# Masked attention on one core: one maximum per key tile over two PSUM banks, and a score ring of two banks

## What is computed

```python
q = xt @ Wq.T                       # one matrix for queries, keys and values
scores = scale * jnp.einsum('bhqd,bhkd->bhqk', qh, qh)
logits = (scores * cmask + (1.0 - cmask) * NEG) * rmask
attn = jax.nn.softmax(logits, axis=-1)
ctx = jnp.einsum('bhqk,bhkd->bhqd', attn, qh)
out = ctx @ Wo.T
return x + transpose(out)
```

## Time and profile before

| | |
|---|---|
| median of 3 runs | 1814.85 us (1810.24 to 1817.87) |
| the profiled execution, its own time | 1814.64 us |
| its span, first to last instruction | 1812.8 us |
| instructions in the profile | 40177 |
| PE busy | 1650.4 us, 91% of the span |
| DVE busy | 1306.6 us, 72% |
| POOL busy | 1207.7 us, 67% |
| ACT busy | 851.5 us, 47% |
| mean granted TensorE clock | 0.954 of full speed |
| HBM traffic over the span | 39 GB/s |

### The profile page before, as it was taken

One profiled execution on the slowest core, in us unless ns is written; L12 is line 12 of the kernel. 1 busy time (PEld: TensorE's weight loads), 2 busy tenths in 40 slices (PEclk: granted clock), 3 DMA queues, 4 the chain that ended last, 5 costly groups with the idle time before them and its releaser, 6 DMA issues.

```text
span 1812.8 us, 40177 instructions
## 1 busy us (share of the span) xinstructions
PE 1650.4 (91%) x10956; PEld 1260.7 (70%) x10956; DVE 1306.6 (72%) x2839; ACT 851.5 (47%) x2055; POOL 1207.7 (67%) x1030
## 2 busy tenths in 40 slices
PE   6688989999999999989899998999999899999995
PEld 4566767677767777767767777677776677777763
DVE  5358677786857768696776968678685877769663
ACT  1135455454635545364544636445463554546451
POOL 5357776758667675777757677675866767586752
PEclk8689999999999999999999999999999999999997
DMA  3234353434434353443434434253443434344410
GB/s 102 71 83 116 91 129 78 129 80 116 111 87 118 76 135 86 104 121 92 119 71 127 97 103 120 69 137 77 122 102 89 116 81 131 83 117 103 103 48 27
DMA packets 93863, 179.70 MB, mean 99 GB/s; under 512 B 24704, under 2 KB 24832, under 8 KB 93632
## 3 DMA queue, kind: packets, MB, share of 16 engines
q1 hardware_dynamic: 64448, 109.71, 26.4%
q0 software_dynamic: 29184, 67.17, 12.8%
HBM read 36.77 MB, written 33.55 MB: 39 GB/s over the span
## 4 chain that ended last, share of the span: by engine, by line
PE 61%; DVE 23%; issue 10%; POOL 2%; ACT 2%; DVEq 1%; SPq 0%; DMA 0%; ACTq 0%; POOLq 0%
PE misc L1087 19%; PE ctx_psum L1054 12%; PE max_scores L1026 8%; DVE small_mxp L828 8%; PE scores L1041 6%; DVE small_xsum L823 5%; PE scores L1044 5%; DVE small_rsum L858 3%; PE misc L1145 3%; PE misc L1113 3%; DVE small_ctx L879 2%; DVE small_xcT_lo L850 1%; PE misc L1135 1%; PE misc L1099 1%; PE misc L1133 1%
## 5 line engine op out<-in xcount | busy, mean ns | idle before, releaser
L828 DVE TENSOR_REDUCE small_mxp<-max_scores 108x1 f32<-108x270 f32 x1280 | 538.3, 433 | 330.2 <-PE max_scores L1026 299.9
L698 ACT ACTIVATE small_Pt<-scores,small_kbias 108x270 f32<-108x270 f32 x1280 | 552.9, 485 | 451.0 <-PE scores L1044 425.2
L540 POOL TENSOR_TENSOR small_Pacc<-small_Pacc,small_Pt 108x540 f32<-108x540 f32 x384 | 532.1, 1386 | 266.4 <-ACT small_Pt L698 256.5
L1026 PE MATMUL max_scores<-small_ops 128*108 128x270 f32 x1280 | 413.7, 341 | 79.3 <-DVE small_mxp L828 78.4
L1026 PEld LDWEIGHTS max_scores<-small_ops 128*108 128x108 f32 x1280 | 223.8, 178 | 176.2 <-DVE small_mxp L828 110.0
L1054 PE MATMUL ctx_psum<-small_Pt,small_V 108*64 108x270 f32 x2560 | 322.8, 400 | 0.0
L1041 PE MATMUL scores<-small_ops 128*108 128x270 f32 x1280 | 297.4, 305 | 4.8 <-ACT small_Pt L698 3.9
L858 DVE RECIPROCAL small_rsum<-small_rsum 128x67 f32<-128x67 f32 (+1 forms) x512 | 240.5, 530 | 78.3 <-ACT small_rsum L644 78.3
L1044 PE MATMUL scores<-small_ops 128*108 128x270 f32 x1280 | 270.6, 294 | 0.0
L1054 PEld LDWEIGHTS ctx_psum<-small_Pt,small_V 108*64 108x64 f32 x2560 | 190.8, 141 | 113.9 <-issue 10.2
L492 POOL DMA_INDIRECT small_xg<-x_rows,small_idx_cur x160 | 171.1, 1069 | 103.9 <-POOL small_idx_cur L485 63.3
(11 more groups left out here) (104 smaller groups left out, 2234.0 us busy)
## 6 DMA issues: line engine op xcount, KB each, us to landing
small_ops<-small_H SPq DMA_DIRECT2D x512, 135.0 KB, 2.5
small_ops<-small_L SPq DMA_DIRECT2D x256, 135.0 KB, 2.6
small_xg<-x_rows,small_idx_cur POOLq DMA_INDIRECT x160, 3.6
out_rows<-small_xg,small_idx_cur POOLq DMA_INDIRECT x160, 3.4
small_ops<-small_mrow SPq DMA_DIRECT2D x128, 2.1 KB
wq_sb<-wq SPq DMA_DIRECT2D x1, 1024.0 KB, 5.7
woT_sb<-woT SPq DMA_DIRECT2D x1, 1024.0 KB, 8.2
wqT_sb<-wqT SPq DMA_DIRECT2D x1, 1024.0 KB, 10.2
```

Source lines behind the costliest of these rows:

```text
L540: nc.gpsimd.tensor_tensor(acc, other, t["Pt"][:R, p0], ALU.add).then_inc(pacc_step, 1)
L698: nc.scalar.activation(t["Pt"][:R, (NT * h + k) % f.NP, half, :], ST[(2 * (NT * h + k) + half) % 3][:R, 0:H], ACT.Exp, bias=t["kbias"][:R, ...
L828: nc.vector.tensor_reduce(t["mxp"][:R, h % 2, m // 2, m % 2:m % 2 + 1], MX[m % 2][:R, 0:H], AX.X, ALU.max).then_inc(mx_red, 1)
L1026: nc.tensor.matmul(MX[m % 2][:R, 0:H], ops[:, OPA, tile_cols(m // 2)], ops[:, OPB, half_cols(m % 2)], start=True, stop=True).then_inc(mx_r ...
```

## The change

The PSUM banks are shared out anew: two for scores instead of three, three for maxima instead of two, as one tensor. The two halves of a key tile go to neighbouring banks: tile number NT*h + k even takes banks 0 and 1, odd takes banks 2 and 1, so half 1 (O) is always in bank 1 and half 0 (E) changes between 0 and 2. DVE takes one negated maximum per key tile over both banks, 540 columns, straight into the column of `mcol`. The partial maxima `mxp` and their reduction L833 are gone, and so is their semaphore.

The waits: E of tile k waits for the reduction of tile k - 2, O of tile k for that of tile k - 1. The matmul of score half u waits for the exponential of half u - 2. On DVE part a = 0 of a step has no reduction any more; part a = 1 begins with the one of the whole tile. The index table of the start moves from `ST[2]` to `ST[1]`.

```diff
+SCORE_BANKS, MAX_BANKS = 2, 3
+def same_bank_before(u, banks, per_batch):
+    return u - banks if u >= banks else next(v for v in range(-1, -banks - 1, -1) if (per_batch + v - u) % banks == 0)
...
-        ST = [psum(f"scores{i}", [P, 512], F32) for i in range(3)]
-        MX = [psum(f"max_scores{i}", [P, 512], F32) for i in range(2)]
+        ST = [psum(f"scores{i}", [P, 512], F32) for i in range(SCORE_BANKS)]
+        MX = psum("max_scores", [P, MAX_BANKS, 512], F32)
...
-            keep("mxp", [P, 2, f.NT, 2], F32)
...
-                                                     ST[(2 * (NT * h + k) + half) % 3][:R, 0:H], ACT.Exp,
+                                                     ST[(2 * (NT * h + k) + half) % SCORE_BANKS][:R, 0:H], ACT.Exp,
...
-                def reduce_max(s, h, m):
-                    dve.wait_ge(mx_ready, 2 * NT * s + m + 1)
-                    nc.vector.tensor_reduce(t["mxp"][:R, h % 2, m // 2, m % 2:m % 2 + 1], MX[m % 2][:R, 0:H], AX.X,
-                                            ALU.max).then_inc(mx_red, 1)
-                    if m == 2 * NT - 1:
-                        dve.wait_ge(mx_red, 2 * NT * (s + 1))
+                def reduce_max(s, h, k):
+                    left = (NT * h + k) % 2
+                    dve.wait_ge(mx_ready, 2 * (NT * s + k) + 2)
+                    if k == 0:
                         at_least(dve, mT_ready, s - 1)
-                        nc.vector.tensor_reduce(t["mcol"][:R, h % 2, :], t["mxp"][:R, h % 2], AX.X, ALU.max,
-                                                negate=True).then_inc(mcol_done, 1)
+                    nc.vector.tensor_reduce(t["mcol"][:R, h % 2, k:k + 1],
+                                            MX[:R, left:left + 2, 0:H], AX.XY,
+                                            ALU.max, negate=True).then_inc(mx_red, 1)
...
-                                if h < HEADS - 2 or has_next:
-                                    reduce_max(s + 2, h + 2, 2 * k + a)
+                                if a == 1 and (h < HEADS - 2 or has_next):
+                                    reduce_max(s + 2, h + 2, k)
...
-                    at_least(pe, mx_red, 2 * NT * s + m - 1)
-                    nc.tensor.matmul(MX[m % 2][:R, 0:H], ops[:, OPA, tile_cols(m // 2)], ops[:, OPB, half_cols(m % 2)],
+                    at_least(pe, mx_red, NT * s + m // 2 - 1 + m % 2)
+                    nc.tensor.matmul(MX[:R, 1 if m % 2 else 2 * ((NT * h + m // 2) % 2), 0:H], ops[:, OPA, tile_cols(m // 2)], ops[:, OPB, half_cols(m % 2)],
...
-                        banks.append(ST[u % 3])
-                        last_user = u - 3 if u >= 3 else next(v for v in range(-1, -4, -1) if (count + v - u) % 3 == 0)
+                        banks.append(ST[u % SCORE_BANKS])
+                        last_user = same_bank_before(u, SCORE_BANKS, 2 * NT * HEADS)
                         at_least(pe, exp_done, 2 * NT * (s - h) + last_user + 1)
...
-                        pe.wait_ge(mcol_done, s + 1)
+                        pe.wait_ge(mx_red, NT * (s + 1))
```

More of the change, by code:

```diff
@@ L281, in attention_kernel @@
         whi_done, ctx_hi_done = sem("whi_done"), sem("ctx_hi_done")
-        mx_red, mcol_done, mrow_done, lo_done = sem("mx_red"), sem("mcol_done"), sem("mrow_done"), sem("lo_done")
+        mx_red, mrow_done, lo_done = sem("mx_red"), sem("mrow_done"), sem("lo_done")
         ctx_done, xv_done, xsum_step, mask_step = sem("ctx_done"), sem("xv_done"), sem("xsum_step"), sem("mask_step")
@@ L919, in body @@
                 nc.vector.tensor_tensor(t["idx"][:R, 1:],
-                                        ST[2][:R, NTALL:B * NTALL].rearrange("p (b i) -> p b i", b=B - 1),
+                                        ST[1][:R, NTALL:B * NTALL].rearrange("p (b i) -> p b i", b=B - 1),
                                         t["boff"][:R, 1:], ALU.add).then_inc(idx_made, 1)
@@ L924, in body @@
                     if name == "mT":
-                        for m in range(2 * NT):
-                            reduce_max(0, 0, m)
+                        for k in range(NT):
+                            reduce_max(0, 0, k)
                     job(name, arg, bank, -1 if name == "xT" else 0, 1 if name == "xT" else 0, 0)
                     if name == "mT":
-                        for m in range(2 * NT):
-                            reduce_max(1, 1, m)
+                        for k in range(NT):
+                            reduce_max(1, 1, k)
                     if name == "proj" and arg[0] < 2:
@@ L1007, in body @@
                     for i in range(1, group + 1):
-                        order(g * group + i, ST[2], bass.ds((g * group + i) * NTALL, NTALL))
+                        order(g * group + i, ST[1], bass.ds((g * group + i) * NTALL, NTALL))
                 pe.wait_ge(g_kept, KD)
@@ L1033, in scores @@
                         pe.wait_ge(mrow_put[h % 2], 16 * (s2 + 1))
-                    banks, count = [], 2 * NT * HEADS
+                    banks = []
                     for half in range(2):
                         u = 2 * (NT * h + k) + half
-                        banks.append(ST[u % 3])
-                        last_user = u - 3 if u >= 3 else next(v for v in range(-1, -4, -1) if (count + v - u) % 3 == 0)
+                        banks.append(ST[u % SCORE_BANKS])
+                        last_user = same_bank_before(u, SCORE_BANKS, 2 * NT * HEADS)
                         at_least(pe, exp_done, 2 * NT * (s - h) + last_user + 1)
```

## The result

| | before | after |
|---|---|---|
| median | 1816.15 us (4 runs) | 1846.32 us (4 runs, 1843.25 to 1850.85) |
| ratio, 95% interval | | 1.0181 (1.0162 to 1.0200) |
| span of the profiled execution | 1812.8 us | 1841.5 us |
| mean granted clock | 0.954 | 0.973 |
| DVE busy | 1306.6 us | 1227.1 us |

The account below looks back on a forecast made before the run. It took TensorE's own work to set most of the time (PE busy 91%). Terms: 45 + 8 + 2 - 31 - 2 - 8 = +14 us on 1814.6, so 1829 us; range 1815 to 1844, chance 0.48.

Parts of the forecast that it names:

- The merged reduction: On DVE, 640 reductions of 540 columns at 714 ns each; DVE sheds 102 us, worth nothing where it waits for PE.
- The score ring: Two score banks: a score matmul waits for the step before's second exponential, at least 1.44 us per consecutive light step.
- one miss: An isolated light step whose scores come late for want of a bank: 0.37 us lost.
- The misses at (5,0) and (7,0): Half a score miss at each; with a maximum miss at (5,1) and (7,2), 0.45 us each time.
- Together 2.8 us a batch, 45 us over 16: Sum of score and maximum misses in the light steps of a middle batch, applied to all 16 batches.
- 8 for starts: Ten batch starts without a turn of the loop: two more score misses, 0.8 us each time, 8 us lost.
- 2 for the last batch: Last batch has no maxima in heads 6 and 7, so more light steps: 2 us lost.
- more clock falls: Rival: clock might fall in (6,0) to (6,2), one fall a batch costing 27 us: 1856 us; chance 0.10.
- Head 3: DVE takes the output tile sooner; stall and clock falls go: 31 us gained, plus 2 in batches 0 and 1.
- What is late next is ACT: In head 3, ACT's gathered-tile pass limits the gain: copy at about 879.9, row sums 881.3; 1.85 us taken.
- The turn of the loop: At 5 turns with a long wait, 0.6 us gained and an estimated 1.0 for avoided clock falls: 8 us.
- Cancelled: Rival: half the miss costs return, 1815 us; chance 0.16.

Follow-up runs that it names:

- half by half: On the changed kernel, score matmuls reordered: first and second matmul of half 0, then of half 1; 1806.1 us, 0.9967 of before.

## Why the prediction was wrong

The direction held and so did most unit prices; the size, 14 us against 29, did not.

- *The merged reduction.* 714 ns forecast, 716 measured. That it would be worth little by itself: 1 to 3 us with the scores in the old order, 8 to 10 half by half.
- *The score ring.* 1.44 us from S2 to S2 forecast, 1.45 measured; one miss 0.37 us forecast, 0.37 measured at (2,1). For batches 2 to 13 the forecast's terms make 38 us (12 times 2.8, and 0.8 for six starts), and 45.2 were measured. The forecast has no miss between (2,4) and (3,0), 0.38 a batch and 4.5 us in all, although it removes the stall behind it. The misses at (5,0) and (7,0), which it halves, make another 1.7.
- *The step that failed most* is "Together 2.8 us a batch, 45 us over 16", with 8 for starts and 2 for the last batch, 55 in all; it was 67.2. I priced all 16 batches as a middle one. The first has no output tiles and the last no maxima in its last heads, so they have more light steps: 22.0 us in batches 0, 1, 14 and 15, where the terms make some 16. And (6,2) and (7,2) of the last batch lose 4.2 us to two clock falls that come with the score waits; this is the "more clock falls" rival, in heads 6 and 7 of the last batch alone. The Trainium skill, "TensorE: Matmul & The Clock Gate", section "A second HAM failure mode: psum-queue depth-cycling", says that short idles of PE between groups of matmuls, as the PSUM banks are cycled, can make the clock go to and fro. The trace agrees with that in the last batch, at 4.2 us, and shows none of it in the light steps of heads 5 and 6 of the other batches, where the stretch below keeps its clock:

```profile
929.00:934.50 5.50, 5.39 (x38) 3.33 (x39) 5.33 (x8) 2.52 (x7) 3.56 (x3) 1.00 0.56 124
```

- *Head 3.* 33 us forecast with batches 0 and 1, 40.2 measured, and the clock falls went as forecast. The reason given, the order on DVE, is one of two: with the reductions apart and the third bank, head 3 gains 28 us as well.
- *"What is late next is ACT".* Inside head 3 that held: in the time of the kernel before (15.19 us earlier, from S2 of (2,4)) ACT's copy comes at 879.7 for the 879.9 forecast and the row sums at 881.0 for 881.3. But the walk ended there. Behind head 3, DVE is late at (4,1), with its token sums, and the forecast put (4,1) and (4,2) at nothing, without a word on them: 11.7 us measured. Moving three sums gave back 20 us.
- *The turn of the loop and starts.* 8 forecast, 11.5 measured.
- *The range and a rival.* The bounds of the terms, 22 us down and 10 up, make 1807 to 1839 and not the 1815 to 1844 that was given, and half of the miss costs is 28 us, which puts "Cancelled" at 1801 and not at 1815.

So of the 15 us missed, 12 are light steps not counted, 12 are (4,1) and (4,2), 4 the clock at the end, less 7 and 3.5 of gains taken too small and 2.5 of others. The costs were short by 28 us; that the number is only 15 off is owed to gains that were short too.

What stays open: why the order half by half costs time with three score banks is read from waits and lengths of steps and not tested by an edit of its own. What makes the same token sum take 0.68 or 1.63 us was not tried either; the trace has a hint. Of the 144 sums of the changed kernel, the 63 beside which POOL runs no TENSOR_TENSOR take at most 0.74 us each, and of the 81 others 48 take over 1 us, up to 2.37. At 906.26, where the sum took 1.63, POOL was in one (L545) from 905.99 to 907.33. And the last 2 to 3 us of "all others" in the table are not explained.

## What to carry to other kernels

Count a PSUM ring by its closed loop (matmul to first use, all uses of the bank, release, the next matmul): where that is longer than a step, taking a bank away costs the difference in each short step, however idle the engines look. Before giving the bank back, finish one half before starting the other: in this kernel that made two banks as good as three (light steps of 1.09 us against 1.07). And when a stall goes, walk on to the next engine's fixed order behind it, where part of the gain may be standing.

## What was not expected of the hardware

The light steps outside the hardware loop are longer than the same ones inside it: 1.16 against 1.07 us before and 1.53 against 1.45 after. In the last batch the clock fell at 1794.7 although no wait of PE was long: four steps with four matmuls of scores each, and waits of 0.54, 0.63 and 0.54 us between them, went ahead of it. And one order of the same four matmuls helps by 40 us with two banks (1846 to 1806) and costs 14 with three (1813.6 to 1828.0). Why the steps outside the loop are longer is open.
